# An attention and expert kernel: GpSimd sends a batch's rows a period later, and attention's periods are written out

## What is computed

```python
x = x + tanh(g_xattn) * attention(layernorm(x), ctx)        # 16 heads of 8 channels
x = x + tanh(g_ffn) * ffn(layernorm(x))

def ffn(x):                                                 # 32 experts, 6 of them for each token
    scores = sigmoid(x @ w_router)
    combine = weights of the 6 best experts of the 4 best of 8 groups, by scores + corr_bias
    routed = einsum('te,eth->th', combine, expert outputs)
    return routed + silu(x @ sh_gate) * (x @ sh_up) @ sh_down
```

## Time and profile before

| | us |
|---|---|
| median of 3 runs | 532.54 |
| lowest and highest run | 527.44, 533.89 |
| the profiled execution | 529.0 |
| its span | 527.2 |

### The profile page before, as it was taken

One profiled execution on the slowest core, in us unless ns is written; L12 is line 12 of the kernel. 1 busy time (PEld: TensorE's weight loads), 2 busy tenths in 40 slices (PEclk: granted clock), 3 DMA queues, 4 the chain that ended last, 5 costly groups with the idle time before them and its releaser, 6 DMA issues.

```text
span 527.2 us, 12958 instructions
## 1 busy us (share of the span) xinstructions
PE 411.1 (78%) x3581; PEld 260.0 (49%) x3582; DVE 339.0 (64%) x885; ACT 273.9 (52%) x524; POOL 210.9 (40%) x368
## 2 busy tenths in 40 slices
PE   0553696968687796875749369999999999999996
PEld 0422343534333342431324145668777777687775
DVE  8074767788875876858684474546665555665575
ACT  0334676676755664555564232356555655565630
POOL 3430204123736424352162472025555555555560
PEclk9996696888869587795777788999999999999999
DMA  6977655363756245572456449436888878884397
GB/s 212 330 196 202 206 161 171 114 198 108 241 159 226 97 143 178 164 226 96 131 192 184 141 148 323 154 101 194 262 258 265 251 233 263 262 251 135 130 345 294
DMA packets 76734, 104.75 MB, mean 199 GB/s; under 512 B 12630, under 2 KB 57782, under 8 KB 76694
## 3 DMA queue, kind: packets, MB, share of 16 engines
q1 hardware_dynamic: 56886, 70.57, 43.0%
q10 hardware_dynamic: 13712, 15.47, 9.9%
q0 software_dynamic: 6096, 18.23, 9.2%
HBM read 57.33 MB, written 46.91 MB: 198 GB/s over the span
## 4 chain that ended last, share of the span: by engine, by line
PE 43%; DVE 14%; issue 12%; DMA 12%; POOL 5%; SPq 5%; another core or an unknown queue 4%; ACT 3%; ACTq 1%; DVEq 0%; POOLq 0%; PEldq 0%
PE ps L1143 11%; PE ps L1163 8%; DVE nmx L1255 5%; DMA split_weights<-pk 5%; DMA rows_by_expert<-filling 4%; DMA ctxb<-picked_rows 3%; PE ps L959 3%; PE ps L1155 3%; PE ps L1125 3%; PE ps L963 3%; PE ps L1046 2%; PE ps L1070 2%; PE ps L928 1%; DVE rD L1271 1%
## 5 line engine op out<-in xcount | busy, mean ns | idle before, releaser
L1255 DVE TENSOR_REDUCE nmx<-ps 128x4 f32<-128x1024 f32 x64 | 75.8, 1221 | 35.9 <-PE ps L928 32.4
L1143 PE MATMUL ps<-wide,bxT 128*128 x474 | 83.6, 313 | 0.7 <-ACT bxT L837 0.7
L630 POOL DMA_INDIRECT picked_rows<-by,bid x79 | 78.1, 989 | 15.0 <-POOL tick L629 13.4
L680 ACT ACTIVATE wide<-ps 128x1024 f32<-128x1024 f32 x64 | 62.8, 1018 | 36.3 <-PE ps L942 29.9
L1481 DVE SCALAR_TENSOR_TENSOR bh<-ps,bx,bsg 128x176 f32<-128x176 f32 x79 | 31.7, 401 | 62.3 <-ACT bsg L853 34.8
L837 ACT ACTIVATE bxT<-ps 128x512 f16<-128x512 f16 x79 | 47.2, 597 | 44.2 <-PE ps L1125 15.5
L1163 PE MATMUL ps<-wide,bhT 88*128 x474 | 65.1, 272 | 0.2
L959 PE MATMUL ps<-wide,vM 128*32 128x256 f32 x512 | 52.5, 458 | 2.5 <-issue 1.1
L582 POOL DMA_INDIRECT rows_by_expert<-pay,place x48 | 48.9, 1018 | 13.4 <-issue 13.2
L963 PE MATMUL ps<-wide,onesM 128*32 128x256 f32 x512 | 51.5, 444 | 0.7
L1143 PEld LDWEIGHTS ps<-wide,bxT 128*128 128x128 f16 x474 | 43.1, 98 | 17.1 <-issue 1.0
(11 more groups left out here) (210 smaller groups left out, 687.0 us busy)
## 6 DMA issues: line engine op xcount, KB each, us to landing
bx<-rows_by_expert ACTq DMA_DIRECT2D x72, 160.0 KB
split_weights<-pk SPq DMA_DIRECT2D x32, 352.0 KB
wide<-split_weights SPq DMA_DIRECT2D x32, 352.0 KB
raw<-in_L_ffn_gate_w SPq DMA_DIRECT2D x32, 176.0 KB
raw<-in_L_ffn_up_w SPq DMA_DIRECT2D x32, 176.0 KB
raw<-in_L_ffn_down_w SPq DMA_DIRECT2D x32, 176.0 KB
split_weights<-pk SPq DMA_DIRECT2D x32, 176.0 KB
wide<-split_weights SPq DMA_DIRECT2D x32, 176.0 KB
```

The costliest lines, as they stand in the source:

```text
L630: nc.gpsimd.indirect_dma_start(PICKED, bass.IndirectOffsetOnAxis(ap=bid[:, j:j + 1], axis=0), by[:, j, :], None).then_inc(placed[j], 16)
L680: act.activation(Pb[:, u % NP, :, :, :], ring(f"B{u}").rearrange("p (i s t) -> p i s t", i=2, s=KT), ACT.Exp, scale=SCALE).then_inc(emptie ...
L1143: last = pe.matmul(ps[:, buf, 0:2 * M], bxT[:, buf, a, k, :], ring_w[:, bass.ds(given[u] + (2 * k + w) * 2 * M, 2 * M)], start=(n == 0), s ...
L1255: dve.tensor_reduce(nmx[:, :, J, 2 * pair:2 * pair + 2, ROW].rearrange("p c g -> p g c"), ring(f"A{u}").rearrange("p (i c s) -> p i c s", ...
```

## The change

`POOL_TURNS` gets another order: the sends stand behind values and ahead of root, and not behind row. In period n they send batch n-4, not n-3, from period 4 on. Their places were made in the period before. Batch 5, which was sent in period 8, is now sent behind period 8's last job, ahead of root of batch 7. The loop over periods 3 to 6 is gone: all nine periods are written out with constant numbers, on all engines.

```diff
-POOL_TURNS = ["values", "root", "split", "context", "row", "send0", "send1", "send2", "xT"]
+POOL_TURNS = ["values", "send0", "send1", "send2", "root", "split", "context", "row", "xT"]
...
         def periods(eng, period):
 
-            period(0, 0)
-            period(1, 1)
-            period(2, 2)
-            with eng.Fori(0, 2) as t:
-                period(3, t * 2 + 3)
-                period(4, t * 2 + 4)
-            period(7, 7)
-            period(8, 8)
+            for n in range(B + 1):
+                period(n, n)
...
-                    elif job[0:4] == "send" and has(kind, "RK"):
+                    elif job[0:4] == "send" and kind >= 4:
                         k = 2 * int(job[4])
-                        send(n - 3, 1 - par, range(k, k + 2))
+                        send(n - 4, par, range(k, k + 2))
 
             periods(pool, period)
+            send(B - 3, (B - 3) % 2)
             root(B - 1)
```

## The result

The changed kernel takes 527.0 us in the median of 20 runs (524.42 to 529.91); the kernel before took 530.13 us in 20 runs beside them (527.06 to 533.89). The ratio is 0.9934 with a 95% interval of [0.9913, 0.9955], so 3.1 us less, well under 2%. The profiled execution took 528.98 us, its span is 527.1 us.

The account below looks back on a forecast made before the run. No engine is full; attention is a chain of periods, lengthened by TensorE waiting under GpSimd's sends. -14.48 + 6.92 - 0.47 = -8.03 us took the profiled 529.0 to 521.0, so a 524.5 us median; own range 520 to 529, whole range 515 to 541.

Parts of the forecast that it names:

- The hold-ups of n = 4 to 6 go: End of periods 4 to 6: sends slow TensorE's weight loads, so moving them removes VectorE's idle time before the reciprocal, -14.48 us.
- 0.47 us of branch: Start of a period, VectorE's first maximum after ob: removing the loop's branch back saves 0.47 us once, between 0 and 1.5.
- Only the hold-ups of n = 4, 5 and 6 are at stake: Period ends: batches 4 and 5 are sent when they were before, so only these three hold-ups can go, 14.48 us together.
- Root at 9.80 us, +6.92: Start of periods 4 to 7: root, behind the sends, starts 9.80 us after the reciprocal; lateness costs one for one, 6.92 us.
- xn: VectorE's step fed by root, ahead of maxima A2 to A4: comes 1 us after root, with 2 us of idle VectorE before it.
- Row's landing: GpSimd's row waits for the six transfers just issued to land: taken as 0, a cost only from a landing over 9 us late.
- A: Rival: TensorE's hold-up at period ends isn't the sends' and stays, with root late: 539.0 us, up to 543.2; chance 0.18.
- B: Rival: the hold-up goes and the late root at the period's start is absorbed: 517.6 us; chance 0.18.
- C: Rival: the hold-up moves with the sends to the start of periods 4 to 7, four times 4.8 us: 536.8 us; chance 0.13.
- D: Rival: nothing measurable changes, since the sends take the same place in time after all; chance 0.03.

Follow-up runs that it names:

- e5: Kernel before, loop and order kept, with the tick ahead of each batch's six DMAs made a 128x256 operation, so sends start 0.43 us later: 540.14 us, 1.0105 of before.
- e9: Kernel before with its periods written out and the tick made a 128x256 operation, sends otherwise where they were: 540.39 us, 1.0135 of before.
- e2: Changed kernel with send2, the last two of six DMAs, moved behind context: 518.51 us, 0.9725 of the kernel before.
- e3: Changed kernel with send0, the first two DMAs of a batch, put back behind row at the period's end, four behind values: 517.11 us, 0.969 of before.
- e1: Kernel before with only its loop written out, sends where they were: 526.15 us, 0.9864 of before.
- e6: Kernel before with only its periods written out, run again beside the changed kernel on one chip: 524.59 us, 0.9874 of before.
- e7: The changed kernel run again, nothing altered, beside the kernel with only its periods written out: 527.19 us, 0.988 of before.
- e8: Changed kernel in which GpSimd's split waits, from period 4 on, until xn is written: 525.58 us, 0.984 of before.
- e4: Changed kernel with all six sends of a batch moved between context and row: 534.98 us, 1.0001 of the kernel before.
- e10: Changed kernel with send0 and send1, four DMAs, at the period's end behind row, and send2 behind values: 524.85 us, 0.9857 of before.
- e12: Two DMAs left at the period's end and four behind values, run again on another chip: 513.84 us, 0.9639 of the kernel before.

## Why the prediction was right and wrong

The forecast was 524.5 us, 8.0 us less than before; measured were 527.0 us, 3.1 us less. It lies in the forecast's own range of 520 to 529, and in part by luck: the forecast started from the median of three runs, 532.54, and twenty runs gave 530.13, from which the same sum would have led to 522.1. The profiled execution was forecast at 521.0 and took 528.98. The gain is well under half of what was forecast, and the parts agree less well than the total.

- **The hold-ups of n = 4 to 6 go: -14.48 us.** Right as a sum: 4.74, 4.88 and 4.86 us are all gone. Wrong in its cause: "I take the sends for the cause" holds (e5, e9, e2 and e3), but not that moving them was needed. e1 has them where they were and loses the same three. The step that failed was to read the edit on the loop as 0.47 us of branch and to look no further: writing the periods out shifted GpSimd and VectorE by some tenths against each other, and alone it is worth -7.2 us by e1 and -8.9 by e6, where the whole change gave -3.1 and, in e7, -6.3.
- **"Only the hold-ups of n = 4, 5 and 6 are at stake".** Wrong: the end of n = 7, where batch 4 is sent as before, got one of 2.23 us. Period 7 was forecast at about 31.5 us and takes 34.54. A hold-up that comes and goes by tenths of a us should have stood in the bounds for every period in which six DMAs run under the last weighing. That of n = 8 stayed, as said (4.71 and 4.66).
- **Root at 9.80 us, +6.92.** The mechanism is right, the size was off. Root starts at 10.10, 10.12, 10.12 and 10.11 us, because the third and fourth DMA take 1.57 and 1.02 us where the six behind the earlier trace rows, whose 8.10 us the sum took over, had 1.34 and 0.96 (the third starts at 173.95, when VectorE's weight split has run since 173.81). Against the earlier trace rows that is later by 0.97, 2.10, 2.58 and 2.52 us: 8.17 us. That a late root costs about one for one is borne out by e2.
- **xn.** Left out: forecast was that it comes 1 us after root, and it does (180.45 - 179.40), but the split, which waited for its input before, now stands ready right behind root and runs beside it. xn takes 1.15 us in n = 4, 5 and 6, 2.4 us together; e8 shows that the split does it, and that less than half of it reaches the period's length.
- **The sum by what was measured:** -14.48 + 8.17 + 2.4 + 2.23 - 0.47 = -2.15 us, against 2.94 less in periods 4 to 7 and 3.1 in the medians. With xn at the 0.91 us that e8 gives it, the sum is -3.64. The measured values lie between the two. The -0.47 in them is doubtful: VectorE's idle time between ob and the first maximum did fall (from 0.69, 0.22 and 0.28 us at the starts of n = 5 to 7 to 0.04 at most), but it lies ahead of root, whose start the sends now set. Without that term the sums are -1.68 and -3.17.
- **Row's landing.** Forecast at nothing. Row waits up to 2.41 us, and GpSimd has idle time behind it (15.39 us before values above, 11.43 before the tick at the end of n = 7), so nothing is still the likeliest price; no run takes that wait away.
- **The rivals.** A (the hold-up isn't the sends') falls by e9 against e1 and by e3. B (the late root is absorbed) falls by e2. C (the hold-up moves along) is not what the changed kernel does: at the start of n = 5 the largest "issue" before TensorE's loads is 1.25 us, and the kernel before, with no send there, has 1.42 and 1.26 us of idle time at the like places; VectorE has no idle time there that ends by "remote". It is what e4 does, in the middle of a period, and in part e1, at the start. D falls by the order itself. The rule that leads to A, from the Trainium skill, "SBUF — State Buffer", section SBUF: two separate sides, is that the ports of the engines and those of the DMAs are disjoint and neither work slows the other. In this kernel TensorE's issue and what waits for it are late under GpSimd's DMAs (e5 and e9, 5.2 to 5.5 us), so the time isn't A's; whether reads of the SBUF are slowed, which is what the rule speaks of, no run here measured.

**What stays open** is what begins a hold-up. In the kernel before the last weighing's loads end 0.12 and 0.08 us before the third DMA starts in n = 3 and 7, and in e1's n = 4 also 0.08 us before it, and the reciprocal isn't held up; in n = 4 of the kernel before, in n = 7 of the changed one and in n = 4 of e9 TensorE still loads weights when the third starts, and there is one. But in e5 the loads were over 0.43 us before the third DMA, and the releases were held for 5.2 us all the same. So that rule isn't enough. Nor is it the length of the second DMA: it is 0.96 us in n = 4 to 6 of the kernel before, but 1.56 us in n = 4 of e5 and 1.65 at the end of n = 7 of the changed kernel, and all of these are held up; and at the end of n = 5 of e10 the reciprocal is held for 1.58 us though the loads were over 0.09 us before the third DMA, as in its n = 4, where it isn't. The end of a hold-up is clearer where it is a full one: the held work goes on 1.0 to 1.5 us after the last DMA of the row (e5: 173.28 after 172.25; the earlier trace rows: 170.33 after 169.09). But it isn't always so: at the end of n = 7 of the changed kernel the reciprocal goes on at 265.46, while the sixth DMA ends at 267.39, and in n = 4 of e4 VectorE goes on at 152.86, with the last DMA ending at 154.59. That the price grows with the number in a row is so at the ends of n = 4 to 6 (six cost up to 5.44 us, four 0 to 1.58, two nothing), but the number alone doesn't settle it: six in a row cost nothing at the reciprocal in e1 and at most 0.68 us at the end of n = 8 of e3 and e12, while e10's four and two more cost 4.78 there.

The version to keep is e3's: two sends at the end of the period and four behind values, 16.3 and 19.0 us below the kernel before in its two comparisons (0.969 and 0.9639), where the changed one has 0.9934 and 0.988.

## What to carry to other kernels

Don't let more than two or so indirect DMAs of GpSimd follow each other where another engine waits for TensorE (here the last weighing; four at a period's start did no visible harm in e2, e3 and e12): spread them, and look in the trace of every period for idle time that ends by "remote", often some 1 us after the last of them. When an edit is made of two parts, run the harmless-looking part alone first; here writing out a loop was worth more than the change it came with, in all likelihood only because it moved two engines by tenths of a us against each other. Where a wait depends on such a coincidence, its gain isn't a property of the edit: a shift of 0.43 us gave 14 us back.

## What the runs showed that was not expected

- Six indirect DMAs of GpSimd, together 7.5 to 8.1 us long, hold back what waits for TensorE on the other engines, by up to 5.46 us, also where TensorE's own last loads had been issued at their usual pace (e5).
- The second DMA of a row takes 0.96 us when it starts before VectorE's split of the weights and up to 1.66 us when it starts behind it; and VectorE's xn takes 0.35 us or 1.15 us, by whether GpSimd's split starts after or before it.
- Starting the sends 0.43 us later costs 14.2 us (e1 to e9).
